# Keys and queries moved to whole heads for the attention scores of six local-attention layers, values kept as copied

## The chip, the cores and the metric

The kernel runs on one core of a Trainium2 chip. The metric is the device time of one execution in microseconds (us), the lower the better. Everything is float32 unless marked otherwise.

## The reference, cut to what matters

The program has two blocks. The first one is a test-time-training layer followed by a stack of six transformer layers; the second is an attention with relative positions and a mixture of experts. The change touches only the six transformer layers, for 4 sequences of 512 tokens of width 128, 16 heads of width 64 and windows of 32 tokens:

```python
for i in range(DEPTH):                       # 6
    x = attn_layer(shift_tokens(x), Wqkv[i], q_scale[i], k_scale[i], Wo[i]) + x
    x = ffn_layer(shift_tokens(x), ln_g[i], ln_b[i], W1[i], b1[i], W2[i], b2[i]) + x
...
q = l2norm(q) * qs;  k = l2norm(k) * ksc
q = q * cos * scale + rotate_half(q) * sin * scale
k = k * cos * inv + rotate_half(k) * sin * inv
# local_attention: a window of 32 queries against its own and the previous 32 keys
sim = jnp.einsum('bhwie,bhwje->bhwij', bq, bk2) * QK_SCALE
sim = jnp.where(mask, -jnp.finfo(sim.dtype).max, sim)
out = jnp.einsum('bhwij,bhwje->bhwie', jax.nn.softmax(sim, -1), bv2)
```

## The kernel before

**Units, rounds, parts.** One pair of layer and sequence is a *unit* (24 of them, `u`), 32 rounds apart; `rounds` (L719) is an order written out by hand, and each engine walks it in order: in round `r` it does step `s = r - 32u` of every unit that is alive, and of every *part* (a tile of 128 tokens and half of the heads, 8 parts a unit, 192 in all, 4 rounds apart from step 39 on). So at any time the projections of unit `u` stand beside the attention of unit `u-1` and the feed-forward of `u-1` or `u-2`. Steps below are counted from a unit's start. A part's step 0 falls on 39, 43, ... 67; seen from the next unit these are 7, 11, ... 35, and the last part's and the one before it on 35 and 31.

**Projections and rotation, steps 0 to 35.** For each of the 8 groups `p` of 4 heads (keys 0 to 3, queries 4 to 7) TensorE makes two halves of 128 columns (L1111 to L1113): rows 32j to 32j+31 hold the lower (or the upper) half of head j. ScalarE squares them (L1293), VectorE multiplies by the rotary tables (L1421, four operations), GpSimd sums the squares (L1556) and joins the rotated parts (L1562, L1563, signal `made`) right in `kT` or `qT`. The norms of the keys are inverted by VectorE at step 17 and those of the queries at step 33 (`inverse_root`, L217 to L226), the keys' ones go out to DRAM and come back spread over 32 rows a head (`norms_wide`, L957), and VectorE scales the keys in place (L1444, steps 24, 28, 29, 32, signal `k_scaled`).

**Scores.** A head's two halves of 32 rows lie in one place, `[32j, g, half]`, so `part_tensor` takes two matmuls of 32 rows for each window and head, the second added in PSUM (L1211): 64 matmuls a part. In the trace each float32 matmul shows as two instructions, so 128.

**Softmax and values.** VectorE multiplies the scores by the queries' norms (L1486) and takes the largest (L1491); ScalarE takes the exponentials (L1357, 8 operations), VectorE inverts the sums (L1494, part step 3), GpSimd scales (L1577), TensorE turns (L1219, part step 5) and weighs the values (L1229, part step 6, 32 matmuls of tiles 64x64), then mixes the heads (L1237). The values come out of the projection by token (steps 29 to 55), ScalarE copies them to `v_tok` (L1306), and SyncE lays the windows out with 8 or 10 DMAs a tile (`value_windows`, L972 to L977).

**Queues.** All DMAs of the layers are issued by SyncE, in the order of `transformer_sync`, waits included: what stands behind a waiting entry waits too. The feed-forward of a unit follows its last part (steps 80 to 109), and the next layer's shift of the same sequence stands at step 124.

## Time and profile before

| | us |
|---|---|
| median of 3 runs (lowest, highest) | 2512.24 (2499.67, 2514.59) |
| the profiled execution's own time | 2506.73 |
| its span, first to last instruction | 2504.8 |

The profiled execution is 5.5 us below the median and within the spread of the three. Spans, idle times and chains in the rows below are all of that one execution. The engines are PE (TensorE), PEld (its weight loads), DVE (VectorE), ACT (ScalarE), POOL (GpSimd) and SP (SyncE); SPq is SyncE issuing DMAs. "Idle before" is the time in which an engine stood still right before a group of instructions, with what released it.

### The profile page before, as it was taken

The numbers are of one execution on the slowest core, as the hardware profiler recorded it, in microseconds if no ns is written. First come the engines' busy times: TensorE is split into PE (matmuls) and PEld (weight loads), VectorE is DVE, ScalarE is ACT, GpSimd is POOL, SyncE is SP. The second block draws the span as 40 slices with busy tenths as digits, with TensorE's granted clock in tenths as the row PEclk, the third lists the DMA queues.
The fourth block names the chain that finished last, engine by engine and source line by source line (L and its number), as shares of the span: only waits on it lengthen the run. The fifth ranks groups of instructions, "written<-read, shape, count | busy, mean of one in ns | idle before, by whom it ended". The sixth has DMA issues, their size and how long they took to land.

```text
span 2504.8 us, 121652 instructions
## 1 busy us (share of the span) xinstructions
PE 2354.9 (94%) x53677; PEld 1748.5 (70%) x53677; DVE 1717.0 (69%) x3393; ACT 1597.2 (64%) x5036; POOL 1451.3 (58%) x1408
## 2 busy tenths in 40 slices
PE   9958999999999999999999999999888999999967
PEld 8836777777777777677777777777645666666657
DVE  4477788777888888787788788887335555555534
ACT  3226777777777787777777778777625454545422
POOL 1166667656676676566666677665117656656307
PEclk9969999999999999999999999999979999999978
DMA  4013333433333334333343333333216222222136
GB/s 91 15 33 86 79 83 94 97 80 83 91 93 95 82 83 103 83 92 87 80 96 90 80 92 87 87 87 87 54 30 177 49 48 48 48 48 48 31 97 249
DMA packets 230208, 204.60 MB, mean 82 GB/s; under 512 B 133687, under 2 KB 155464, under 8 KB 229552
## 3 DMA queue, kind: packets, MB, share of 16 engines
q1 hardware_dynamic: 225296, 190.91, 30.5%
q8 instruction: 422, 6.91, 1.2%
q0 software_dynamic: 2208, 5.58, 0.7%
q14 instruction: 106, 0.87, 0.1%
q10 hardware_dynamic: 2176, 0.33, 0.1%
HBM read 86.05 MB, written 15.70 MB: 41 GB/s over the span
## 4 chain that ended last, share of the span: by engine, by line
PE 66%; DVE 12%; SPq 6%; ACT 5%; issue 5%; POOL 4%; DMA 3%; POOLq 0%; ACTq 0%; DVEq 0%
PE psum L1211 7%; PE psum L1959 5%; PE psum L1237 5%; PE psum L1229 5%; PE psum L1938 4%; PE psum L1111 4%; PE psum L1944 3%; PE psum L1113 3%; PE psum L1112 3%; PE psum L1993 3%; PE psum L1983 3%; ACT p L1357 3%; SPq L972 3%; PE psum L1188 2%; PE psum L1219 2%
## 5 line engine op out<-in xcount | busy, mean ns | idle before, releaser
L1357 ACT ACTIVATE p<-p,stat 128x64 f32<-128x64 f32 x1536 | 512.4, 336 | 47.2 <-DVE stat L1491 44.9
L1577 POOL TENSOR_TENSOR p<-p,inverse 128x512 f32<-128x512 f32 x192 | 200.2, 1043 | 456.5 <-DVE inverse L1494 452.2
L1211 PE MATMUL psum<-kT,qT 32*32 32x64 f32 x24576 | 305.5, 224 | 25.8 <-issue 24.2
L2092 DVE TENSOR_REDUCE largest<-psum 128x1 f32<-128x512 f32 x256 | 165.0, 687 | 228.0 <-PE psum L1944 228.0
L1211 PEld LDWEIGHTS psum<-kT,qT 32*32 32x32 f32 x24576 | 264.1, 103 | 75.3 <-issue 74.3
L1357 ACT ACTIVATION_READ_ACCUMULATOR p<-p,stat 128x1 f32 x1536 | 288.6, 188 | 0.0
L1421 DVE SCALAR_TENSOR_TENSOR rotated<-psum,scales,rotary 128x512 f32<-128x512 f32 x384 | 270.8, 742 | 25.8 <-ACT sq L1293 25.8
L1556 POOL TENSOR_TENSOR squares<-sq 128x512 f32<-128x512 f32 x192 | 245.3, 1278 | 44.3 <-ACT sq L1293 43.8
L1293 ACT ACTIVATE sq<-psum 128x512 f32<-128x512 f32 x384 | 213.7, 582 | 57.3 <-PE psum L1113 54.6
L1229 PEld LDWEIGHTS psum<-pT,v_win 64*64 64x64 f32 x12288 | 198.6, 136 | 64.7 <-issue 45.9
L1111 PE MATMUL psum<-xs,wqkv_high 128*128 128x512 f32 x384 | 205.7, 536 | 23.2 <-DVE rotated L1421 22.9
L2014 ACT ACTIVATE w_by_key<-psum 128x512 f32<-128x512 f32 x128 | 76.4, 597 | 230.1 <-PE psum L1959 230.1
L1229 PE MATMUL psum<-pT,v_win 64*64 64x32 f32 x12288 | 220.1, 221 | 2.8 <-ACT pT L1363 1.8
L1237 PEld LDWEIGHTS psum<-oT,wo 128*128 128x128 f32 x1536 | 187.9, 196 | 38.5 <-issue 26.3
L1237 PE MATMUL psum<-oT,wo 128*128 128x128 f32 x1536 | 198.2, 283 | 9.0 <-ACT oT L1368 5.6
L1363 ACT ACTIVATE pT<-psum 128x512 f32<-128x512 f32 x192 | 114.2, 595 | 130.4 <-PE psum L1219 130.3
L1306 ACT ACTIVATE v_tok<-psum 128x512 f32<-128x512 f32 x192 | 113.8, 593 | 101.8 <-PE psum L1113 73.9
L1444 DVE TENSOR_TENSOR kT<-kT,rnorm_wide 128x1024 f32<-128x1024 f32 x96 | 164.0, 1728 | 13.4 <-DMA rnorm_wide<-rnorms 13.3
L2104 POOL TENSOR_TENSOR q_by_head<-q_heads,mask_head 64x256 fp32r<-64x256 f32 x252 | 157.5, 625 | 15.4
L2060 ACT ACTIVATE weights<-psum,largest 128x512 f32<-128x512 f32 x256 | 161.5, 687 | 3.7 <-DVE largest L2092 3.7
L1421 DVE SCALAR_TENSOR_TENSOR kT<-psum,scales,rotary 128x512 f32<-128x512 f32 x192 | 142.3, 741 | 28.2 <-ACT sq L1293 14.4
L1563 POOL TENSOR_TENSOR qT<-qT,rotated 128x512 f32<-128x512 f32 x96 | 157.9, 1645 | 0.0
(351 smaller groups left out, 5402.3 us busy)
## 6 DMA issues: line engine op xcount, KB each, us to landing
v_win<-v_tok SPq DMA_DIRECT2D x576, 128.0 KB
rnorm_wide<-rnorms SPq DMA_DIRECT2D x384, 64.0 KB
v_win<-v_tok SPq DMA_DIRECT2D x336, 64.0 KB
q_rows<-q_rows_all SPq DMA_DIRECT2D x32, 512.0 KB, 4.6
tile_weights<-expert_table SPq DMA_DIRECT2D x23, 512.0 KB, 5.8
wqkv<-L_ffn_Wqkv SPq DMA_DIRECT2D x96, 64.0 KB, 2.2
rel_values<-sq SPq DMA_DIRECT2D x60, 64.0 KB, 2.2
wo<-L_ffn_Wo SPq DMA_DIRECT2D x48, 64.0 KB
```

What stands on the lines that cost most here:

```text
L1111: PE.e.matmul(out, w[0], x[1], start=True, stop=False)
L1211: last = PE.e.matmul(psum[WIN * blk:WIN * (blk + 1), f, out], q[rows, g, half, tok:tok + WIN], k[rows, g, half, tok:tok + 2 * WIN], start= ...
L1229: last = PE.e.matmul(psum[to:to + DH, 2 + o, at:at + WIN], v[rows, blk, 2 * (2 * a + o) + h, :], t.pt[h][rows, 2 * a + o, blk * WIN:(blk + ...
L1237: last = PE.e.matmul(ps[:, 0:P], t.wo[:, e, :], t.ot[e % 2][:, e // 2, :], start=(e == 0), stop=(e == PAIRS - 1))
L1293: A.e.activation(t.sq[half][:, :], c.psum[:, 4 + half, :], ACT.Square).then_inc(*t.squared.by((u, (p, half))))
L1357: last = A.e.activation(p, p, ACT.Exp, bias=t.stat[:, h, 2 * g + f:2 * g + f + 1], accum_out=t.sum[:, h, g, f:f + 1])
L1421: last = V.e.scalar_tensor_tensor(out=rot[x], in0=psum[:, 4 + half, :], scalar=scale, in1=table, op0=ALU.mult, op1=ALU.mult)
L1444: V.e.tensor_tensor(k, k, t.wide[g % 2][:, :].unsqueeze(1).to_broadcast([P, 2, S]), ALU.mult).then_inc(*t.k_scaled.by((u, g)))
L1556: G.e.tensor_tensor(t.sq_both[p % 2][:, :], t.sq[0][:, :], t.sq[1][:, :], ALU.add).then_inc(*t.squares.by((u, p)))
L1577: G.e.tensor_tensor(p, p, t.inv[:, h, :, :].unsqueeze(3).to_broadcast([P, GROUPS_TF, 2, 2 * WIN]), ALU.mult).then_inc(*t.p_scaled.by(m))
L2060: A.e.activation(t.e[n % 4][:, :], c.psum[:, n % 5, :], ACT.Exp, bias=t.mx[n % 4][:, 0:1]).then_inc(*t.exped.by(n))
L2092: V.e.tensor_reduce(t.mx[n % 4][:, :], psum[:, n % 5, :], AX, ALU.max, negate=True).then_inc(*t.largest.by(n))
```

## The change

- **Scores over 64 rows.** `q` and `k` now hold whole heads: rows 64f to 64f+63 are one head, both halves. A window and head takes one matmul of 64 rows and 32 columns of weights: 32 a part. Which of two banks a head's scores go to depends on the window too (`swapped`).
- **Staging and relay.** Rotated queries are made in six staging buffers, and the keys' scaling writes its product there, one operation for each half. `relay` moves each group's two halves from staging to the whole heads with 4 DMAs (64 rows of 2 KB each) on SyncE: 8 relays a unit. The first score of a unit waits for the last of them; VectorE waits for a relay six buffers back before it writes a staging buffer.
- **Norms.** One DMA instead of four spreads the norms of a group. The steps of spreading and scaling move (the third scaling from 29 to 32, the last from 32 to 33, behind the queries' `inverse_root` of step 33).
- **Values.** ScalarE copies the values straight into `v_win`; odd windows use that copy as it is, the others a second copy made by 4 or 6 DMAs a tile. For that, half of the heads' values come from tokens whose 64-halves are exchanged (`swap_halves`: four copies on GpSimd at step 28). The order of the weighing matmuls follows `swapped`. Values move from steps 29 to 33, their DMAs from 31 to 37.
- **The rest.** The feed-forward starts 4 steps later; the copy of the queries' norms takes 3 operations; squares use three buffers; `pT` has one.

```diff
--- before.py
+++ after.py
@@ -712,20 +712,21 @@
-VALUE_FIRST, WINDOWS_AT = 29, 31
+VALUE_FIRST, WINDOWS_AT, SWAP_AT = 33, 37, 28
 SHIFT_AT = -4
-SQUARES_LAG, SUM_LAG, MADE_LAG = 2, 4, 3
-NORM_AT = {"root0": 17, "out": 15, "root1": 33, "turn": 39, "copy": 39}
-SPREAD_AT = (16, 18, 19, 24)
-SCALE_AT = (24, 28, 29, 32)
+SQUARES_LAG, SUM_LAG, MADE_LAG, RELAY_LAG = 2, 4, 3, 4
+NORM_AT = {"root0": 17, "out": 19, "root1": 33, "turn": 39, "copy": 39}
+SPREAD_AT = (20, 20, 26, 29)
+SCALE_AT = (24, 28, 32, 33)
+STAGES, WIDES = 6, 2
...
-FFN_AT = {"shift": 80, "center": 83, "square": 84, "sum": 84, "root": 84, "spread": 88, "scale": 89, "gate0": 91, "gate1": 95, "gate2": 96, "gelu": 99,
-          "up0": 100, "up1": 101, "up2": 104, "down": 108, "add": 109}
+FFN_AT = {"shift": 84, "center": 87, "square": 88, "sum": 88, "root": 88, "spread": 92, "scale": 93, "gate0": 95, "gate1": 99, "gate2": 100, "gelu": 103,
+          "up0": 104, "up1": 105, "up2": 108, "down": 112, "add": 113}
 NORM_SPREAD, NORM_SCALE = 2, {1: 9, 2: 17, 3: 25}
 NORM_ENDS = (0, B - 1)
 TABLES = (2, 3, 0, 1)
-UNIT_STEPS = 110
-SPLIT_AT = {2: 13, 3: 31, 0: 39, 1: 40, 4: 56, 5: 59}
+UNIT_STEPS = 118
+SPLIT_AT = {2: 13, 3: 31, 0: 39, 1: 40, 4: 60, 5: 62}
...
+def swapped(f, blk):
+
+    return f if blk < TPB // 2 else 1 - f
+
+
+def squares_at(u, p, half=0):
+
+    return (2 * GROUPS_TF * u + p + half) % 3
+
+
+def stage_of(u, kind, g, half):
+
+    turn = [(1, 0), (1, 1), (0, 0), (1, 2), (0, 1), (1, 3), (0, 2), (0, 3)].index((kind, g))
+    return (2 * GROUPS_TF * u + turn) * 2 + half
+
+
+def relayed_on(t, k):
+
+    return t.relayed[k % STAGES].on((k, 1))
+
+
 def made_of(t, u, kind, g):

-    return [t.q[u % 2][:, g, half, :] if kind else t.k[u % 2][:, g, half, WIN:WIN + S] for half in range(2)]
+    if kind:
+        return [t.stage[stage_of(u, 1, g, half) % STAGES][:, :] for half in range(2)]
+    return [t.k[u % 2][:, g, half, WIN:WIN + S] for half in range(2)]
...
+            for g in range(GROUPS_TF):
+                if s == 4 * (GROUPS_TF + g) + RELAY_LAG:
+                    SP.wait_ge(*t.made.on((u, GROUPS_TF + g)))
+                    relay(c, t, u, 1, g)
+                if s == SCALE_AT[g] + 1:
+                    SP.wait_ge(*t.k_scaled.on((u, g)))
+                    relay(c, t, u, 0, g)
...
 def norms_wide(c, t, u, g):

+    SP, x = c.SP, GROUPS_TF * u + g
+    SP.wait_ge(*t.rn_out.on(u))
+    if x >= WIDES:
+        SP.wait_ge(*t.k_scaled.on(divmod(x - WIDES, GROUPS_TF)))
+    src = bass.AP(t.rn_dram[u % 2].tensor, g * S, [[GROUPS_TF * S, 4], [0, HALF_D], [1, S]])
+    SP.e.dma_start(t.wide[x % WIDES][:, :], src).then_inc(*t.wide_in[x % WIDES].by(x))
+
+
+def relay(c, t, u, kind, g):
-    SP.wait_ge(*t.rn_out.on(u))
-    if u or g >= 2:
-        SP.wait_ge(*t.k_scaled.on((u, g - 2) if g >= 2 else (u - 1, GROUPS_TF + g - 2)))
-    for j in range(4):
-        src = bass.AP(t.rn_dram[u % 2].tensor, (j * GROUPS_TF + g) * S, [[0, HALF_D], [1, S]])
-        SP.e.dma_start(t.wide[g % 2][HALF_D * j:HALF_D * (j + 1), :], src).then_inc(*t.wide_in[g % 2].by((u, g, j)))
+    if u >= 2:
+        SP.wait_ge(*t.scored.on((u - 1) * PARTS - 1))
+    for half in range(2):
+        k = stage_of(u, kind, g, half)
+        for e in range(2):
+            to = t.q[u % 2][half::2, g, e, :] if kind else t.k[u % 2][half::2, g, e, WIN:WIN + S]
+            SP.e.dma_start(to, t.stage[k % STAGES][e * H64:(e + 1) * H64, :]).then_inc(*t.relayed[k % STAGES].by((k, e)))


...
-    SP, v, vt, v_in = c.SP, t.v[n % 2], t.vt[n % 2], t.v_in[n % 2]
+    SP, v, before, v_in = c.SP, t.v[n % 2], t.v[(n - 1) % 2], t.v_in[n % 2]
     SP.wait_ge(*t.v_kept.on((n, 1)))
     if n >= 2:
         SP.wait_ge(*t.weighted.on(2 * (n - 2) + 1))
-    k = 0
-    for f in range(2):
-        at = f * 2 * WIN
-        for blk in range(1, TPB):
-            SP.e.dma_start(v[at:at + 2 * WIN, blk, :, :], vt[(blk - 1) * WIN:(blk + 1) * WIN, f, :, :]).then_inc(*v_in.by((n, k)))
-            k += 1
-        SP.e.dma_start(v[at + WIN:at + 2 * WIN, 0, :, :], vt[0:WIN, f, :, :]).then_inc(*v_in.by((n, k)))
-        k += 1
-        if n % TPB:
-            SP.e.dma_start(v[at:at + WIN, 0, :, :], t.vt[(n - 1) % 2][P - WIN:P, f, :, :]).then_inc(*v_in.by((n, k)))
-            k += 1
+    w0, w1, w2, w3 = (slice(WIN * w, WIN * (w + 1)) for w in range(TPB))
+    SP.e.dma_start(v[WIN:P, 1, 0, :, :], v[0:P - WIN, 0, 0, :, :]).then_inc(*v_in.by((n, 0)))
+    SP.e.dma_start(v[w1, 1, 1, :, :], v[w0, 0, 1, :, :]).then_inc(*v_in.by((n, 1)))
+    SP.e.dma_start(v[w0, 1, 1, :, :], v[w3, 0, 1, :, :]).then_inc(*v_in.by((n, 2)))
+    SP.e.dma_start(v[w3, 1, 1, :, :], v[w2, 0, 1, :, :]).then_inc(*v_in.by((n, 3)))
+    if n % TPB:
+        SP.e.dma_start(v[w0, 1, 0, :, :], before[w3, 0, 0, :, :]).then_inc(*v_in.by((n, 4)))
+        SP.e.dma_start(v[w2, 1, 1, :, :], before[w1, 0, 1, :, :]).then_inc(*v_in.by((n, 5)))
...
+        if f:
+            PE.wait_ge(*t.swapped.on(u))
+        tokens = [x[:, i * P:(i + 1) * P] for x in (t.xp if f else xs)]
+        three_products(PE, ps, tokens, w).then_inc(*t.valued.by((u * TPB + i, f)))
...
-        PE.wait_ge(*t.k_scaled.on((u, GROUPS_TF - 1)))
-        PE.wait_ge(*t.made.on((u, 2 * GROUPS_TF - 1)))
+        for back in range(STAGES):
+            PE.wait_ge(*relayed_on(t, 4 * GROUPS_TF * (u + 1) - 1 - back))
...
-            for half in range(2):
-                for blk in range(TPB):
-                    tok, out = i * P + blk * WIN, slice(g * 2 * WIN, (g + 1) * 2 * WIN)
-                    for f in range(2):
-                        j = 2 * h + f
-                        rows = slice(HALF_D * j, HALF_D * (j + 1))
-                        last = PE.e.matmul(psum[WIN * blk:WIN * (blk + 1), f, out], q[rows, g, half, tok:tok + WIN], k[rows, g, half, tok:tok + 2 * WIN],
-                                           start=False, stop=(half == 1 and g == GROUPS_TF - 1))
+            for blk in range(TPB):
+                tok, out = i * P + blk * WIN, slice(g * 2 * WIN, (g + 1) * 2 * WIN)
+                for f in range(2):
+                    rows = slice(DH * f, DH * (f + 1))
+                    last = PE.e.matmul(psum[WIN * blk:WIN * (blk + 1), swapped(f, blk), out], q[rows, g, h, tok:tok + WIN], k[rows, g, h, tok:tok + 2 * WIN],
+                                       start=False, stop=(g == GROUPS_TF - 1))
...
-                        rows, to, at = slice(DH * f, DH * f + DH), (f + o) % 2 * DH, a * P + blk * WIN
-                        last = PE.e.matmul(psum[to:to + DH, 2 + o, at:at + WIN], v[rows, blk, 2 * (2 * a + o) + h, :],
-                                           t.pt[h][rows, 2 * a + o, blk * WIN:(blk + 1) * WIN], start=True, stop=True)
+                        slot, to, at = swapped(f, blk), (f + o) % 2 * DH, a * P + blk * WIN
+                        rows = slice(DH * slot, DH * slot + DH)
+                        last = PE.e.matmul(psum[to:to + DH, 2 + swapped(o, blk), at:at + WIN], v[rows, 1 - blk % 2, f, 2 * (2 * a + o) + h, :],
+                                           t.pt[rows, 2 * a + o, blk * WIN:(blk + 1) * WIN], start=True, stop=True)
...
-        A.e.activation(t.rq[u % 2][:, :, :].rearrange("p b r -> p (b r)"), ring_bank(c, t, "unit", u, "rn")[:, 0:P], ACT.Copy).then_inc(*t.rn_kept.by(u))
+        norms = ring_bank(c, t, "unit", u, "rn")[:, 0:P]
+        A.e.activation(t.rq[u % 2][0:H64, :, :].rearrange("p b r -> p (b r)"), norms[0:H64, :], ACT.Copy)
+        pairs = lambda x: x.rearrange("p (b a h f g) -> p b a h f g", b=TPB, a=2, h=2, f=2)
+        for f in range(2):
+            last = A.e.activation(pairs(t.rq[u % 2][H64:P, :, :].rearrange("p b r -> p (b r)"))[:, :, 1, :, 1 - f, :], pairs(norms[H64:P, :])[:, :, 1, :, f, :], ACT.Copy)
+        last.then_inc(*t.rn_kept.by(u))
...
+        if kind:
+            for half in range(2):
+                if stage_of(u, kind, g, half) >= STAGES:
+                    V.wait_ge(*relayed_on(t, stage_of(u, kind, g, half) - STAGES))
...
-    if s in SCALE_AT:
-        g = SCALE_AT.index(s)
-        k = t.k[u % 2][:, g, :, WIN:WIN + S]
-        V.wait_ge(*t.wide_in[g % 2].on((u, g, 3)))
-        V.wait_ge(*t.made.on((u, g)))
-        V.e.tensor_tensor(k, k, t.wide[g % 2][:, :].unsqueeze(1).to_broadcast([P, 2, S]), ALU.mult).then_inc(*t.k_scaled.by((u, g)))
+    for g in range(GROUPS_TF):
+        if s == SCALE_AT[g]:
+            x = GROUPS_TF * u + g
+            V.wait_ge(*t.wide_in[x % WIDES].on(x))
+            V.wait_ge(*t.made.on((u, g)))
+            for half in range(2):
+                k = stage_of(u, 0, g, half)
+                if k >= STAGES:
+                    V.wait_ge(*relayed_on(t, k - STAGES))
+                last = V.e.tensor_tensor(t.stage[k % STAGES][:, :], t.k[u % 2][:, g, half, WIN:WIN + S], t.wide[x % WIDES][:, :], ALU.mult)
+            last.then_inc(*t.k_scaled.by((u, g)))
...
+    if s == SWAP_AT:
+        if u:
+            G.wait_ge(*t.valued.on((u * TPB - 1, 1)))
+        for k in range(2):
+            for to, x in swap_halves(t, u, k):
+                last = G.e.tensor_copy(to, x)
+        last.then_inc(*t.swapped.by(u))
```

## Rows read from the trace of the kernel before

**Rows 1.** The page: busy time by engine, and the chain that ended last

```profile
PE 2354.9 (94%) x53677; PEld 1748.5 (70%) x53677; DVE 1717.0 (69%) x3393; ACT 1597.2 (64%) x5036; POOL 1451.3 (58%) x1408
...
PE 66%; DVE 12%; SPq 6%; ACT 5%; issue 5%; POOL 4%; DMA 3%; POOLq 0%; ACTq 0%; DVEq 0%
```

**Rows 2.** Busy time by stretch, 600 to 1400 us (inside the layers)

```profile
core 0: us, PE busy (x) PEld busy (x) DVE busy (x) ACT busy (x) POOL busy (x), PEclk, DMA share, GB/s
600.00:1400.00 800.00, 777.63 (x21274) 582.74 (x21257) 645.90 (x1263) 619.02 (x2149) 531.39 (x417) 1.00 0.36 90
```

**Rows 3.** One line's instructions: the copy of norms, one a unit

```profile
L1298 ACT ACTIVATE rnorm_tok<-psum x24: 268/278/280, 188.3 to 1753.1; 128x128 f32<-128x128 f32 x24
```

**Rows 4.** Groups by line, 600 to 1400 us: count | busy us, mean ns | idle before

```profile
L1211 PE MATMUL psum<-kT,qT 32*32 32x64 f32 x11995 | 148.5, 223 | 10.9 <-issue 10.0
...
L1229 PE MATMUL psum<-pT,v_win 64*64 64x32 f32 x5952 | 105.7, 220 | 0.9 <-issue 0.9
```

**Rows 5.** Instructions of L1211 within 904.6 to 905.2 us

```profile
L1211 PE MATMUL psum<-kT,qT x58: 212/214/238, 904.6 to 905.2; 32*32 32x64 f32 x58
```

**Rows 6.** PE in order of time: start us, length us, what

```profile
913.04 1.48 PE L1211 MATMUL psum<-kT,qT 32*32 32x64 f32 x128
914.45 1.12 PE L1180 MATMUL psum<-sq,w 128*128 128x512 f32 x2
...
918.97 1.14 PE L1229 MATMUL psum<-pT,v_win 64*64 64x32 f32 x64
920.04 0.50 PE L1111 MATMUL psum<-xs,wqkv_high 128*128 128x512 f32 x1
...
926.02 0.66 PE L1219 MATMUL psum<-ident,p 128*128 128x128 f32 x4 [1.01 <-POOL p L1577]
...
931.57 0.39 PE L1203 MATMUL psum<-maskb,identb 128*128 128x256 bf16 x2
```

**Rows 7.** DVE in order of time, steps 27 to 34 of one unit

```profile
907.04 0.68 DVE L1486 TENSOR_TENSOR p<-psum,rnorm_tok 128x512 f32<-128x512 f32 x1
909.07 0.29 DVE L1498 TENSOR_TENSOR z<-z,psum 128x128 f32<-128x128 f32 x1 [1.34 <-PE psum L1237]
...
909.87 4.20 DVE L1444 TENSOR_TENSOR kT<-kT,rnorm_wide 128x1024 f32<-128x1024 f32 x2
913.99 0.19 DVE L1494 RECIPROCAL inverse<-sum 128x8 f32<-128x8 f32 x1
...
918.01 1.22 DVE L1444 TENSOR_TENSOR kT<-kT,rnorm_wide 128x1024 f32<-128x1024 f32 x1
919.14 0.28 DVE L1431 TENSOR_TENSOR norms<-psum,norms 128x128 f32<-128x128 f32 x1
...
924.64 0.20 DVE L1494 RECIPROCAL inverse<-sum 128x8 f32<-128x8 f32 x1
```

**Rows 8.** ACT: the last of eight exponentials between those two inverses

```profile
912.47 0.34 ACT L1357 ACTIVATE p<-p,stat 128x64 f32<-128x64 f32 x1
```

**Rows 9.** POOL: joining group 6 (step 27), scaling; then all casts of L2161

```profile
908.44 1.28 POOL L1563 TENSOR_TENSOR qT<-qT,rotated 128x512 f32<-128x512 f32 x1
...
924.92 1.04 POOL L1577 TENSOR_TENSOR p<-p,inverse 128x512 f32<-128x512 f32 x1 [3.28 <-DVE inverse L1494]
...
L2161 POOL CAST keys<-k x16: 396/448/507, 1870.9 to 2322.5; 128x256 fp32r<-128x256 f32 x8, 128x384 fp32r<-128x384 f32 x8
```

**Rows 10.** SyncE issuing DMAs, in order of time

```profile
904.05 2.19 SPq L972 DMA_DIRECT2D v_win<-v_tok  x3
...
907.56 2.69 SPq L972 DMA_DIRECT2D v_win<-v_tok  x3
...
910.93 0.59 SPq L977 DMA_DIRECT2D v_win<-v_tok  x1
...
922.69 2.78 SPq L972 DMA_DIRECT2D v_win<-v_tok  x3
```

**Rows 11.** DMAs issued, 600 to 1400 us: count, KB each, us to landing

```profile
v_win<-v_tok SPq DMA_DIRECT2D x280, 128.0 KB
...
wqkv<-L_ffn_Wqkv SPq DMA_DIRECT2D x48, 64.0 KB, 2.2
```

**Rows 12.** PE near the end of the layers, in order of time

```profile
1828.95 2.07 PE L1173 MATMUL psum<-ident,rstd 128*128 128x128 f32 x8 [2.42 <-DVE rstd L226]
1832.38 5.49 PE L1180 MATMUL psum<-sq,w 128*128 128x512 f32 x6 [1.36 <-DVE sq L1459]
```

79 lines of the change are left out of this document (44 added, 35 removed).

## The prediction

> **What bounds the kernel now.** First the page: TensorE is busy for 94% of the span and carries 66% of the chain that ended last; the reader is to see that no other engine carries more than 12% of it [rows 1]. Then the layers alone, from 600 to 1400 us: of 800 us TensorE is busy 777.6 (97%), VectorE 645.9 (81%), ScalarE 619.0 (77%), GpSimd 531.4 (66%), the DMA engines 36%, at a granted clock of 1.00, which is the 2.4 GHz level [rows 2]. So the layers are bound by TensorE on average, but VectorE has only a fifth of its time left. The period of a unit is (1753.1 - 188.3) / 23 = 68.0 us [rows 3], and 24 units make nearly 1640 us: 1 us a unit is 24 us, almost 1% of the whole.
>
> Then one unit in order of time, because the shares hide where the slack lies. In steps 27 to 34 VectorE lags: the third and second scaling take 4.20 us together beside GpSimd's work, against 1.22 us for one that runs alone, and the queries' inverse root runs from about 919.4 to 924.6 [rows 7]. Only then comes the inverse of a part's sums at 924.64, GpSimd's scaling at 924.92 [rows 9], and TensorE's turn at 926.02, for which it stood still for 1.01 us [rows 6]. From that turn to the next unit's first score, at 931.57, TensorE needs 5.55 us [rows 6]. I call steps 27 to 39 the heavy half (score 27 to score 39); the rest of the unit has room beside TensorE.
>
> **The change, part by part.** *Scores.* 11995 instructions are 93.7 parts; their 148.5 us busy and 10.9 us of waits for instructions make 1.70 us a part [rows 4], 1.41 at least (913.04 to 914.45) [rows 6]. The new part has 64 instructions. Bounds: 64 instructions at the rate of the first 58 of an old part, 0.6 us [rows 5], or half of 1.41, 0.70; above, what the 64 instructions of the weighing take, 1.07 (918.97 to 920.04) [rows 6], with weights of 64 columns, where the new scores keep 32. Moving columns (64) and tiles in use at once (8) stay as they are, so I take 0.85, nearer the lower end, and leave half of the 0.29 us of excess, 0.15: 1.00. Saved: 0.70 us a part.
>
> *Weighing.* Same 32 matmuls, but `swapped` turns their order round after the second window: the tile used last is wanted again at once, three times a part. The rows show no such case. Below it costs nothing (the same tiles and columns); above, each waits for one whole round of four tiles, 1.07 / 8 = 0.13, so 0.4. It could gain nothing, since no operand shrinks. I take 0.10, nearer nothing, for two instructions of a tile already follow each other. Net on TensorE: 0.60 us a part, 4.8 a unit, 115 in all, if all of it reached the end.
>
> Here the trace leaves something open: the weighing lets two row tiles write to one bank, in different rows, and its 64 instructions still take 17 ns each [rows 6], but this may be its weights' loading or that sharing. The Trainium skill, TensorEngine Tiling (Array Packing), Restrictions and Gotchas, says that different row tiles can't access one PSUM bank at the same time. The old scores kept each row tile to its own bank; the new ones let both into each. By that rule the new part would not reach 0.85; it is the third rival below.
>
> *VectorE.* Two scalings of 512 columns for one of 1024: at least 1.22 us, at most half of 4.20 = 2.10 [rows 7]; I take 1.7 for a pair. In the unit shown: the mix ends 0.75 earlier (one shorter score ahead of it), so the sum z starts at 908.3 and the maximum ends at 909.2; one scaling instead of two ends at 910.9; the exponentials, which ended at 912.8 [rows 8], end 0.7 sooner, so the inverse stands at 912.3 instead of 913.99 [rows 7]. From there the old order runs 4.0 us to the scaling at 918.01: 916.3. The third scaling (now step 32) ends at 918.0, the norms and the inverse root last 5.5 (919.14 to 924.64): 923.5. The last scaling, now behind the root, ends at 925.2, and the part's inverse comes at 925.3, 0.7 later than before. GpSimd and the turn follow: 926.7, plus 5.55 = 932.3 for the first score, against 931.57 [rows 6]. So the heavy half gains nothing and loses about 0.7 us, although TensorE has three shorter scores in it. What hid VectorE there was TensorE's own work; the cover is gone. Between 930.5 (every scaling at 1.22) and 933.2 (at 2.1) lies -1.1 to +1.6.
>
> *GpSimd.* The exchange at step 28 is four copies of 128x256, 0.45 us each by the casts of such tiles [rows 9], 1.6 to 2.1 us. It stands behind group 6's joining, which ends at 909.7, and ahead of the next unit's shift; a part's scaling would run from about 915 instead of 914.3. Behind it wait the joining of group 7 and its relay, and the turn of step 32: 1 us late for TensorE, which catches up before the turn of step 36 that waits anyway. It costs nothing extra.
>
> *SyncE and DMA.* A unit issues 32 relay DMAs, 4 for norms, 22 for values and 1: 59, before 16 + 38 + 1 = 55. From step 28 to the first score, 27 come in one row: relays of queries 2 (4), values (6), keys 1 (4), norms (1), queries 3, keys 2, keys 3 (12). Ten such issues took 904.05 to 911.52, 0.75 us each [rows 10]; 27 take 20.2 from 909.7 (joining of group 6 done) [rows 9]: 929.9. A DMA lands 2.2 us after its issue starts [rows 11], so 1.6 after the issue ends: 931.5, just ahead of the 932.3 of VectorE's path. It is hidden by 0.8 us. Bytes: values from 992 KB a tile to about 480, relays add 4.2 MB a unit; net +2 MB on 6.1, with the engines 36% busy [rows 2], so some 48% after: no bound. Value DMAs at step 37 instead of 31 still stand 8 steps ahead of their use.
>
> *Light half.* Five scores of the eight lie in it (39 to 55). 5 x 0.60 = 3.0 us saved, at TensorE's pace, since VectorE, ScalarE and GpSimd have room there. The copies on ScalarE for the norms (two more, at most 0.28 each [rows 3]) hide.
>
> *Ends.* Four more steps leave part of one feed-forward uncovered at the end (stalls of 2.42 and 1.36 us show how thin work is there [rows 12]); the first unit waits for its relays. 3 us in all, 0 to 8.
>
> **Sum.** Unit: -3.0 + 0.7 = -2.3; 24 units: -55; ends +3: -52. From the profiled execution's own 2506.7 that is 2455; the median of the runs is 5.5 above that execution, so 2460 for the median.
>
> **The rivals.**
> 1. *All of TensorE's saving arrives*: VectorE's path in the heavy half is not the tight one, because its waits shrink too. For it: 97% busy TensorE, a stall of only 1.01 us at the turn. Against it: the sum above. 24 x 4.8 = 115, +3: 2395 + 5.5 = 2400.
> 2. *The relays come late*, and the kernel gets slower. Place: SyncE's 27 issues ahead of step 39. Three issues of 64 rows have taken 2.78 us, 0.93 each [rows 10]; if all were like these, 909.7 + 25.0 + 1.6 = 936.3, 4.7 later than 931.57. The unit changes by 4.7 - 3.0 = +1.7: +41, +3: 2551, with the 5.5, 2556. It decides from where the last relay lands 3 us after 931.57, at 0.87 us an issue. Against it: ten issues in a row averaged 0.75.
> 3. *Row tiles in one bank exclude each other.* Every second pair of windows would wait for the pair ahead: 0.35 us more a part in the scores and weighing. Light half 5 x 0.25 = 1.25, less 0.7: -0.55 a unit, -13, +3: 2497, with the 5.5, 2502. This is the rule of the Trainium skill named above (TensorEngine Tiling, Gotcha 1). For it: 17 ns an instruction in the weighing. Against it: weights of 64 columns explain these as well.
> 4. *The change doesn't do what it says*, for the halves are twice handled: excluded as a whole by the instruction counts, which the diff fixes; that its cover fails in small places (exchange, ring of squares, one `pT`) gives about 2500.
>
> **How the numbers follow.** Chances: the forecast 0.45, rival 1 0.20, rival 2 0.14, rival 3 0.13, rival 4 0.08. About 1% (25 us) is what a measurement of this kernel can tell from no change, so faster means below 2487 and slower above 2537. Faster: forecast 0.43, rival 1 0.20, rival 3 0.03: 0.66. Slower: rival 2 beyond 2537, 0.13. Same: the rest, 0.21. The range reaches from rival 1 (2400, less 5 for its own spread) to 2515, past rivals 3 and 4; outside are rival 2 and the lucky end of rival 1. The forecast's own range, from the heavy half's -1.1 to +1.6 us and a part's saving of 0.45 to 0.75, is 2420 to 2500.
>
> **What would show it.** Right: 64 instructions a part at about 0.85 us; a unit of 65.7 us; TensorE busy some 93% in the layers instead of 97%, standing still for 2 to 3 us before the turn of step 36 (released by GpSimd's scaling behind VectorE's inverse); VectorE near 84%; the last relay landing shortly before the first score. Wrong: the first score released by a DMA (rival 2), scores of over 1.1 us a part (rival 3), a TensorE still 97% busy with a unit near 63 us (rival 1). The sum would fail most easily at the light half, if there, too, the chain score, maximum, exponentials, inverse, scaling, turn left no room once TensorE is quicker.

## The result, and the profile after

| | before | after |
|---|---|---|
| median of 4 runs each (lowest, highest), us | 2510.60 (2499.67, 2514.59) | 2760.84 (2759.70, 2768.23) |
| span of the profiled execution, us | 2504.8 | 2759.1 |
| granted clock of TensorE, mean | 0.966 | 0.917 |

The ratio is 1.101, 95% interval 1.097 to 1.105: the changed kernel is 10% slower, +250 us, or 10.4 us for each of the 24 units. The prediction had 2460 us. Below, one point is 1% of the time before, 25 us; gains and losses are given in points of the ratio to the kernel before on the same chip, because its median moved by 0.6% between the groups of runs (2495.2 to 2511.0). One execution of e12 and one of e16 were in a slower state and are left out of medians and ratios.

The page of the kernel after: busy time by engine, then the chain that ended last. It answers [rows 1].

```profile
PE 2360.0 (86%) x41389; PEld 1701.2 (62%) x41389; DVE 1720.7 (62%) x3489; ACT 1607.0 (58%) x5106; POOL 1457.0 (53%) x1503
...
PE 37%; ACT 15%; DVE 13%; SPq 12%; DMA 10%; POOL 7%; issue 5%; another core or an unknown queue 0%; ACTq 0%; DVEq 0%; POOLq 0%
```

Every engine is busy for almost the same time as before, in a span 254 us longer. TensorE had 66% of the chain and has 37%; what it lost went to ScalarE, to SyncE's issues and to DMAs in flight. So no engine became the bound: the engines wait for each other.

The same in the layers (busy time by stretch, columns as in [rows 2]), and one stretch of 5 us inside them:

```profile
600.00:1400.00 800.00, 685.61 (x13183) 490.72 (x13182) 556.40 (x1131) 540.62 (x1894) 459.61 (x398) 0.91 0.42 102
940.00:945.00 5.00, 0.84 (x4) 0.84 (x5) 1.35 (x3) 2.47 (x5) 1.28 (x1) 0.56 0.72 195
```

TensorE is busy for 686 us of 800 instead of 778, the granted clock is 0.91 instead of 1.00. It fell where TensorE stood: from 940 to 945 us it worked for 0.84 of 5 us, and the mean grant was 0.56. TensorE stood from 939.6 to 944.2; the grant was 0.80 from 940 to 941, 0.50 (the level of 1.2 GHz) from 941 to 947, and 1.00 again from 948.

TensorE's work is thus stretched too. Its busy time of 2360.0 us looks like that of before, but it now has 41389 matmul instructions instead of 53677. The kernel of e4 below has the same 41389 and is busy for 2233.0 us, at a mean grant of 0.971 instead of 0.917. So up to 127 us of TensorE's busy time in after are work at the lower clock. How much of that reaches the end was not measured, and each price below contains its share of it.

TensorE in order of time around the scores of one part (`L1262`) and a weighing (`L1281`), which answer [rows 6]:

```profile
890.51 1.14 PE L1281 MATMUL psum<-pT,v_win 64*64 64x32 f32 x64
891.58 0.50 PE L1155 MATMUL psum<-xs,wqkv_high 128*128 128x512 f32 x1
...
892.70 0.86 PE L1262 MATMUL psum<-kT,qT 64*32 64x64 f32 x64
893.49 0.33 PE L1190 MATMUL psum<-ident,rnorm 128*128 128x128 f32 x1
```

And the new copies of norms, two a unit, from which the period of a unit follows as in [rows 3]:

```profile
L1362 ACT ACTIVATE rnorm_tok<-psum x48: 179/187/194, 194.4 to 2004.1; 64x32 f32<-64x32 f32 x48
```

(2004.1 - 194.4) / 23 = 78.7 us a unit, before 68.0. The 10.7 us are the result: (78.7 - 68.0) x 24 = 257 us, about the whole of the 254 us that the span grew. The loss lies in every unit, not at the ends.

What the engines wait for, 600 to 1400 us (engine, line, what it waited for: us in all, times, the longest):

```profile
ACT v_win L1372 <- DMA v_win<-v_win: 51.0, 10, 6.5
...
PE psum L1289 <- ACT oT L1435: 35.0, 10, 5.1
...
DVE stage L1519 <- DMA rnorm_wide<-rnorms: 9.7, 10, 2.7
...
PE psum L1256 <- DMA kT<-stage: 6.8, 3, 3.3
```

Some ten units lie in that stretch. Once a unit ScalarE waits 5 us for the DMAs that lay out the tile of values before, and TensorE 3.5 us at the mix for ScalarE's copy (`oT`) that stands behind. Before, the same wait was

```profile
ACT v_tok L1306 <- DMA v_win<-v_tok: 11.7, 6, 4.1
```

The first score of a unit, `L1256`, is held by a relay only three times (6.8 us). The chain of the work that ended last, in one of those places (start us, us, what):

```profile
925.96 1.24 POOL stage L1643
927.22 0.53 SPq L1004
...
930.90 0.58 SPq L990
...
932.19 0.59 SPq L1016
...
934.81 0.59 SPq L1021
935.44 6.99 DMA v_win<-v_win
...
959.32 5.34 DMA rnorm_wide<-rnorms
```

GpSimd joins a group of queries, SyncE issues its relay (`L1004`), the spreading of norms (`L990`) and the windows of a tile of values (`L1016` to `L1021`), which then take 7.0 us to land. The stretch in which the clock fell, 940 to 945 us, is the one in which ScalarE waits for them and TensorE for ScalarE (in order of time; the bracket is idle time before, with what ended it):

```profile
939.18 0.39 PE L1157 MATMUL psum<-wqkv_high,x_swapped 128*128 128x512 f32 x1
944.16 3.59 PE L1289 MATMUL psum<-oT,wo 128*128 128x128 f32 x16 [4.59 <-ACT oT L1435]
```

A DMA of norms takes 5.3 us. The prediction had given a landing 2.2 us [rows 11].

### The profile page after: what moved, and what is told of

Its sections match the earlier page's. It is cut to its first block, busy times and chain, and to the rows that moved or that the text cites. A ratio compares the mean times of both kernels' runs of the same rounds, so it can differ in the third digit from the quotient of the medians.

```text
span 2759.1 us, 97721 instructions
## 1 busy us (share of the span) xinstructions
PE 2360.0 (86%) x41389; PEld 1701.2 (62%) x41389; DVE 1720.7 (62%) x3489; ACT 1607.0 (58%) x5106; POOL 1457.0 (53%) x1503
## 4 chain that ended last, share of the span: by engine, by line
PE 37%; ACT 15%; DVE 13%; SPq 12%; DMA 10%; POOL 7%; issue 5%; another core or an unknown queue 0%; ACTq 0%; DVEq 0%; POOLq 0%
ACT p L1424 6%; SPq L1004 6%; DMA v_win<-v_win 5%; PE psum L2039 5%; PE psum L2018 4%; DMA rnorm_wide<-rnorms 3%; PE psum L2024 3%; DVE rotated L1492 3%; PE psum L1289 3%; PE psum L2073 3%; PE psum L2063 3%; PE psum L1235 2%; POOL stage L1642 2%; POOL stage L1643 2%; ACT sq L1353 1%
## 5 line engine op out<-in xcount | busy, mean ns | idle before, releaser
L1289 PE MATMUL psum<-oT,wo 128*128 128x128 f32 x1536 | 231.4, 313 | 97.6 <-ACT oT L1435 92.6
L1289 PEld LDWEIGHTS psum<-oT,wo 128*128 128x128 f32 x1536 | 217.7, 224 | 128.9 <-ACT oT L1435 112.8
L1281 PEld LDWEIGHTS psum<-pT,v_win 64*64 64x64 f32 x12288 | 210.8, 143 | 78.1 <-issue 46.0
L1155 PE MATMUL psum<-xs,wqkv_high 128*128 128x512 f32 x384 | 221.4, 576 | 28.9 <-DVE rotated L1492 28.5
L1281 PE MATMUL psum<-pT,v_win 64*64 64x32 f32 x12288 | 232.5, 227 | 9.4 <-ACT pT L1430 9.4
L1270 PE MATMUL psum<-ident,p 128*128 128x128 f32 x768 | 130.3, 296 | 116.9 <-POOL p L1657 61.6
L1372 ACT ACTIVATE v_win<-psum 128x512 f32<-128x512 f32 x192 | 114.6, 597 | 158.9 <-DMA v_win<-v_win 118.8
L1570 DVE RECIPROCAL inverse<-sum 128x8 f32<-128x8 f32 x192 | 38.3, 199 | 252.8 <-ACT p L1424 252.8
L1270 PEld LDWEIGHTS psum<-ident,p 128*128 128x128 f32 x768 | 95.9, 153 | 160.2 <-POOL p L1657 154.6
L1519 DVE TENSOR_TENSOR stage<-kT,rnorm_wide 128x512 f32<-128x512 f32 x192 | 170.7, 930 | 29.2 <-DMA rnorm_wide<-rnorms 29.0
L1353 ACT ACTIVATE sq<-psum 128x512 f32<-128x512 f32 x256 | 147.1, 584 | 45.7 <-PE psum L1157 43.7
L1262 PE MATMUL psum<-kT,qT 64*32 64x64 f32 x12288 | 168.1, 227 | 0.0
```

The costliest lines, as they stand in the source:

```text
L1155: PE.e.matmul(out, w[0], x[1], start=True, stop=False)
L1262: last = PE.e.matmul(psum[WIN * blk:WIN * (blk + 1), swapped(f, blk), out], q[rows, g, h, tok:tok + WIN], k[rows, g, h, tok:tok + 2 * WIN] ...
L1270: last = PE.e.transpose(psum[:, 2, g * P:(g + 1) * P], t.p[h][:, g, :, :].rearrange("p f k -> p (f k)"), c.ident[:, :])
L1281: last = PE.e.matmul(psum[to:to + DH, 2 + swapped(o, blk), at:at + WIN], v[rows, 1 - blk % 2, f, 2 * (2 * a + o) + h, :], t.pt[rows, 2 * a ...
L1289: last = PE.e.matmul(ps[:, 0:P].rearrange("p (x q) -> p x q", x=2), t.wo[:, e, :], mixed_rows(t, e % 2, e // 2), start=(e == 0), stop=(e = ...
L1353: A.e.activation(t.sq[squares_at(u, p, half)][:, :], c.psum[:, 4 + half, :], ACT.Square).then_inc(*t.squared.by((u, (p, half))))
```

## The experiments

Eighteen kernels with edits, all on one core. One unit's 8 parts start at steps 7, 11, ... 35 of the next unit. Behind the experiments stands a table of the mean time from each part's first mask matmul (`L1203`) to the next one's. It is worked out from the starts of those instructions over 20 units.

### The norms in one DMA

The kernel after, with the norms of a group spread by four DMAs as before:

```diff
-    src = bass.AP(t.rn_dram[u % 2].tensor, g * S, [[GROUPS_TF * S, 4], [0, HALF_D], [1, S]])
-    SP.e.dma_start(t.wide[x % WIDES][:, :], src)...
+    for j in range(4):
+        src = bass.AP(t.rn_dram[u % 2].tensor, (j * GROUPS_TF + g) * S, [[0, HALF_D], [1, S]])
+        SP.e.dma_start(t.wide[x % WIDES][HALF_D * j:HALF_D * (j + 1), :], src)...
```

> The kernel after with one edit: the norms of a group are spread by four DMAs of 32 rows each, as in the kernel before, instead of by one whose source has the dimensions 4, 32, 512. Same bytes, three more issues of about 0.45 us for each group on SyncE. Theory A (the one norms DMA is served by few DMA engines, so it lands after 5 us, and whatever stands behind it in their rings lands late too: the 7.0 us landing of the value windows and the 5.3 us landing of the norms in the chain of the kernel after): the 10 us a unit that were lost come back, about 2480 us (2440 to 2530). Theory B (the 32 relay DMAs a unit and their 4.2 MB fill the rings, whatever form the norms take): no gain, 2740 to 2800 us, for SyncE issues 12 DMAs a unit more.

The opposite, the kernel before with one DMA for a group:

> The kernel before with one edit: the norms of a group are spread by one DMA with the dimensions 4, 32, 512, as in the kernel after; steps, scores and values stay. Theory A: slower than before though SyncE has 12 issues a unit less, by the share of the loss that doesn't need relays behind it: 2550 to 2700 us. Theory B: 2500 to 2515 us, no change or slightly faster.

Measured: after with four, 2706.0 us, ratio 1.085 (1.082 to 1.087), where after has 1.101: 1.6 points, 41 us, come from this one DMA. That is a sixth of the loss, where theory A expected all of it and theory B none. Before with one: 2515.7 us, 1.009 (1.006 to 1.013), 23 us slower although it issues 12 DMAs less a unit, so B is out and A's 2550 to 2700 us is missed too. A stretch of that kernel in which a DMA of norms was all that was in flight (columns as in [rows 2]):

```profile
975.00:976.00 1.00, 0.63 (x24) 0.59 (x25) 1.00 (x2) 0.86 (x4) 0.00 (x0) 1.00 0.26 102
```

The DMA engines' share is 0.26, about 4 of 16. The source pattern is [4, 32, 512]: the Trainium skill, DMA: Bandwidth & Descriptors, How many engines (k), says that a DMA is laid on the largest number of engines, up to 16, that divides the slowest dimension of its source and of its target, and this row agrees for 4. No run here has the same bytes with the dimensions in another order. VectorE pays, in that kernel and in the one before (waits, 600 to 1400 us):

```profile
DVE kT L1443 <- DMA rnorm_wide<-rnorms: 27.8, 19, 2.7
```

```profile
DVE kT L1444 <- DMA rnorm_wide<-rnorms: 6.6, 6, 1.6
```

Why it costs 41 us in after and 23 in before was not measured. In after the relays and the DMAs of values stand behind it in a longer row; whether they queue on the same four engines is open.

### The scores alone

The kernel before with only its loop of scores changed (heads come out mixed: the data stays where it was, the shapes are those of after):

```diff
-            for half in range(2):
-                ... rows = slice(HALF_D * j, HALF_D * (j + 1)); matmul(..., q[rows, g, half, ...], k[rows, g, half, ...])
+                    rows = slice(DH * f, DH * (f + 1))
+                    last = PE.e.matmul(psum[WIN * blk:WIN * (blk + 1), f, out], q[rows, g, h, tok:tok + WIN], k[rows, g, h, tok:tok + 2 * WIN], ...)
```

> The kernel before with only the scores changed: 32 matmuls of 64 rows a part instead of 64 of 32 rows, each row tile in its own bank as before. It leaves out the move to whole heads, so it multiplies rows of different heads and its result is another one; the work of every other engine and all waits stay. It measures what TensorE's saving is worth with nothing added. If all of it arrives (0.62 us a part by the trace of the kernel after, where 64 instructions and the way to the next take 0.79 us against 1.41): 192 x 0.65 = 125 us less, 2385 us. If VectorE's path through steps 27 to 39 sets that half, as predicted: five of eight parts, 75 us less, 2435 us.

Measured: 2456.3 us, 0.984 (0.982 to 0.986): 1.6 points, 40 us. The group of scores and the waits, 600 to 1400 us:

```profile
L1209 PE MATMUL psum<-kT,qT 64*32 64x64 f32 x6208 | 83.5, 224 | 0.0
```

```profile
PEld psum L1217 <- POOL p L1575: 42.3, 36, 2.3
PEld psum L1235 <- ACT oT L1366: 40.1, 48, 1.4
```

97 parts at 0.86 us, against 148.5 / 93.7 = 1.58 [rows 4], and 10.9 / 93.7 = 0.12 us of waits for instructions are gone too. Neighbouring groups overlap, so TensorE's busy time falls by less, by 122 us in the whole kernel (2354.9 to 2233.0) or 0.64 a part. With the waits that is about 0.75 a part, near the 0.70 predicted, and 145 us over 192 parts; a good quarter of it arrives. Both expectations, all of it (2385 us) and five eighths (2435 us), are missed.

TensorE now stands at the turn (`L1217`) for GpSimd's scaling and at the mix (`L1235`) for ScalarE's copy, and not only in the heavy half: by the starts in the trace, over 20 units, 3.8 of these 7.1 us a unit lie before step 27. So the chain scores, maximum, exponentials, inverse, scaling, turn, with the mix behind it, limits TensorE in the light half too. That it does so in every part isn't shown: the turn waits 36 times in 97 parts.

### The relays

The kernel with four DMAs of norms (e1), without relays from the third unit on; with relays of 64 columns instead of 512; with half of each relay's DMAs:

```diff
+                if u >= 2:
+                    continue            # e5
...
+            n = S if u < 2 else 64      # e6
...
-        for e in range(2):
+        for e in range(2 if u < 2 else 1):   # e7
```

> The kernel of e1 (norms in four DMAs) without relays and without waits for them from the third unit on; it leaves out the move of keys and queries to whole heads there, so its scores are those of stale rows. Everything else of the change stays: 64-row scores, exchange on GpSimd, values straight into their windows, queries' norms ahead of the last scaling. Theory C (SyncE's one queue: 32 relay issues a unit stand ahead of norms and value windows, and those come late): nearly all of e1's loss goes, 2450 to 2490 us. Theory E (the direct copy of values, which now waits for the previous tile's windows five steps after their issue, or the exchange on GpSimd, or the scaling behind the root, is itself the loss): 2550 to 2700 us.

> The kernel of e1 with all its relays issued and waited for, but from the third unit on with 64 instead of 512 columns a row: the same number of issues and packets, an eighth of the bytes; most of each row isn't moved, so the scores are wrong. Theory C (issue time on SyncE): as e1, 2690 to 2715 us. Theory D (the bytes in the DMA rings, landing late): as e5.

> The kernel of e1 with two of the four DMAs of each relay from the third unit on: half of the issues and half of the bytes, one half of the heads isn't moved. Theory C: 16 issues of 0.65 us less in a unit whose queue is the chain; half of the loss against e5 or more goes, 2540 to 2620 us, and clearly below e6. Theory D: between e6 and e1, no lower than e6.

With all relays of queries issued by GpSimd, right behind its joining:

> The kernel of e1 with the queries' relays (16 DMAs a unit) issued by GpSimd right behind the operation that makes them, the keys' still by SyncE; all of the result is computed. Theory C: SyncE's queue is relieved of half of the relays, 2550 to 2650 us, unless GpSimd's own issue (about 1 us each for the indirect DMAs it issues in the last stage) delays its scalings; then 2650 to 2800 us. Theory D: as e1, 2690 to 2715 us.

Measured: without relays 2654.8 us, 1.064 (1.062 to 1.065), 2.1 points or 53 us less than e1's 1.085. Short relays 2689.7, 1.078 (1.076 to 1.080): the bytes are 0.7 points, the issues and their places the rest. Half the DMAs 2657.8, 1.065 (1.062 to 1.068): the second half, issues and bytes, costs 49 us, the first 4. So it isn't a fixed price per DMA. That everything behind the row is late from some length on fits this, and no run varied the length further. Moving the queries' issues to GpSimd, 2697.9, 1.081 (1.079 to 1.083), takes back 0.4 points.

Theory C (SyncE's row) has the direction in e5 to e7 and too much of the size: of the 216 to 256 us it expected in e5, 53 came, and e7 and e8 miss its ranges as well. Theory E (another part of the change is the loss; 2550 to 2700 us in e5) fits e5, and the next two groups of runs follow it. Theory D (the bytes alone) is out by e6. In e1, where the norms' DMA is no longer in the way, the relays do hold the first score of nearly every unit; in e8 no engine waits for a relay or a window any more, and TensorE waits for GpSimd's scaling instead, for GpSimd is busy for 563 us of 800 there and 479 in e1 (waits, 600 to 1400 us: e1, e1, e8):

```profile
PE psum L1257 <- DMA kT<-stage: 20.2, 9, 4.4
PE psum L1271 <- POOL p L1658: 23.6, 15, 2.6
```

```profile
PE psum L1274 <- POOL p L1664: 60.5, 25, 5.6
```

### The exchange of the values' halves

e5 with `swap_halves` for the first unit only:

```diff
-    if s == SWAP_AT:
+    if s == SWAP_AT and u == 0:
```

> The kernel of e5 (no relays from the third unit on, norms in four DMAs) that also exchanges the halves of the tokens only for the first unit, so half of the values of later units come from stale tokens. Theory G (GpSimd's four copies at step 28, 1.6 us in e5's trace, stand with the shift of 2.3 us ahead of a part's scaling and make TensorE wait): 2590 to 2620 us against e5's 2655. Theory F (the later feed-forward and values set the loss): no more than 10 us less, 2645 to 2655 us.

Measured: 2617.3 us, 1.049 (1.048 to 1.051): 1.4 points, 36 us, or 1.5 us a unit. The four copies in e5 (lines, 600 to 1400 us: count | busy, mean ns):

```profile
L1635 POOL CAST x_swapped<-xs 128x256 fp32r<-128x256 f32 x44 | 20.4, 503 | 0.0
```

They take 0.50 us each, 2.0 a unit, and 1.5 us a unit reach the end, as theory G expected (2590 to 2620 us).

### What is left: later steps alone, in the kernel before

e9 is still 4.9 points, 123 us, slower than before, with shorter scores, without relays and exchange. What remains of the change are steps in other places. Each was made alone in the kernel before:

```diff
-FFN_AT = {"shift": 80, "center": 83, ...}; SPLIT_AT = {..., 4: 56, 5: 59}
+FFN_AT = {"shift": 84, "center": 87, ...}; SPLIT_AT = {..., 4: 60, 5: 62}     # e10
-VALUE_FIRST, WINDOWS_AT = 29, 31
+VALUE_FIRST, WINDOWS_AT = 33, 37                                             # e11: e10 and this
-SPREAD_AT = (16, 18, 19, 24); SCALE_AT = (24, 28, 29, 32); "out": 15
+SPREAD_AT = (20, 21, 26, 29); SCALE_AT = (24, 28, 32, 33); "out": 19          # e12 (the second spreading at 21; after has 20)
```

> The kernel before with only the feed-forward's steps 4 later and the last two weight splits at 60 and 62, as in the kernel after. Theory F1 (the gelu, with its two table loads 4.2 us on ScalarE, now falls on step 103, a round that is also a unit's first score with the copy of its norms, and the exponentials behind it come late): slower than before, 2560 to 2620 us. Otherwise within 10 us of 2497 us.

> The kernel before with the steps of the change for values (33, their DMAs 37) and for the feed-forward, nothing else: same operations, same DMAs. Theory F2 (the schedule itself, values and feed-forward together, is the loss, because their copies now meet the exponentials): 2600 to 2660 us, most of what e5 has over before. If the direct copy of values and the exchange are the loss: below 2540 us.

> The kernel before with only the steps of the norms moved as in the change: the DMA out at 19, their spreading at 20, 21, 26, 29, the scalings at 24, 28, 32, 33, the last behind the queries' inverse root. The prediction's own term: the part's inverse 0.7 us later in the heavy half, TensorE not faster here: 0.5 to 1.5 us a unit, 2510 to 2535 us. If VectorE's order doesn't matter: 2490 to 2505 us.

| kernel before with | us | ratio (95%) |
|---|---|---|
| feed-forward 4 later, splits moved (e10) | 2690.0 | 1.079 (1.077 to 1.081) |
| that, and values at 33, their DMAs at 37 (e11) | 2868.9 | 1.150 (1.148 to 1.153) |
| scalings late, nearly as in after (e12) | 2504.8 | 1.004 (1.003 to 1.005) |

The edit that the prediction put at nothing but "ends" is the largest of those made alone, and larger than expected (2560 to 2620 us). Values late cost 7 points more in the old arrangement, with its 38 window DMAs a unit, again beyond what was expected (2600 to 2660 us); ScalarE's copy of values waits 131 us of 800 for these DMAs there. In after there are 22, and what moving the values costs there was not measured alone. The scalings cost 10 us, 0.4 a unit, below the 0.5 to 1.5 expected.

### Which part of the feed-forward's move

The steps of the feed-forward 4 later, the splits where they were; 8 later; 4 later with the queries' norms turned and copied at step 37 instead of 39, and that same step in e1:

```diff
-FFN_AT = {"shift": 80, ... "gelu": 99, ...}
+FFN_AT = {"shift": 84, ... "gelu": 103, ...}     # e13
+FFN_AT = {"shift": 88, ... "gelu": 107, ...}     # e15
-"turn": 39, "copy": 39
+"turn": 37, "copy": 37                           # e14: e13 and this; e16: e1 and this
```

> The kernel before with the feed-forward 4 steps later and nothing else (weight splits stay at their steps; in e10 they moved too, to 60 and 62, behind the point at which values at step 29 need them). Theory H (the gelu's 4.2 us on ScalarE meets the queries' norms and a unit's first score on step 39): most of e10's loss stays, 2590 to 2650 us. Theory I (in e10 the splits that came late were the loss, about 8 us at each of five layer borders and more behind them): below 2530 us.

> The kernel of e13 with the turn and the copy of the queries' norms at step 37 instead of 39, so ahead of the gelu on ScalarE. Theory H in its narrow form (VectorE's first scores and TensorE's ring wait for that copy behind the gelu, 1.9 and 2.4 us in the trace of e10): 50 to 90 us less than e13. If the exponentials behind the second table load are what is late: no more than 20 us less.

> The kernel before with the feed-forward 8 steps later instead of 4, nothing else. The mixes and the sums of squares come every 8 steps, so against them it stands as before, and its gelu falls on step 107, so 43, away from the copy of the norms. Theory H: within 30 us of the kernel before, 2490 to 2525 us. If any later feed-forward costs because its work meets other parts: 2600 us or more.

> The kernel of e1 (the change with the norms in four DMAs) with the turn and the copy of the queries' norms at step 37, all of the result computed. Theory H, narrow: 30 to 90 us less than e1's 2706, 2620 to 2675 us. If exponentials or SyncE's queue set the end there anyway: 2690 us or more.

| kernel | us | ratio (95%) |
|---|---|---|
| before, feed-forward 4 later (e13) | 2675.8 | 1.066 (1.064 to 1.068) |
| e13 and norms copied at 37 (e14) | 2677.6 | 1.065 (1.063 to 1.067) |
| before, feed-forward 8 later (e15) | 2600.7 | 1.035 (1.034 to 1.037) |
| e1 and norms copied at 37 (e16) | 2722.0 | 1.084 (1.082 to 1.086) |

Four steps later costs 6.6 points, 165 us, eight steps only 3.5: the tail isn't it, for it would grow. It is the neighbourhood. The other 1.3 points of e10 are the splits of the weights, which come too late there for values at step 29 at each of the five layer borders (e10, 600 to 1400 us, three borders):

```profile
PE psum L1111 <- POOL wqkv_low L1569: 21.0, 3, 7.3
```

ScalarE in e13, in order of time (start us, us, what), with the gelu at its new step 103, which is step 39 of the unit after the next:

```profile
1006.84 1.28 ACT L1345 ACT_TABLE_LOAD   x1
1008.14 1.67 ACT L1345 ACTIVATE act<-act 128x512 f32<-128x512 f32 x3
1009.71 0.25 ACT L1298 ACTIVATE rnorm_tok<-psum 128x128 f32<-128x128 f32 x1
...
1011.38 0.58 ACT L1363 ACTIVATE pT<-psum 128x512 f32<-128x512 f32 x1
1011.98 1.28 ACT L1357 ACT_TABLE_LOAD   x1
```

TensorE and VectorE in the same stretch; the bracket is idle time before, with what ended it:

```profile
1010.02 1.12 PE L1183 MATMUL psum<-sq,w 128*128 128x512 f32 x2 [2.38 <-ACT rnorm_tok L1298]
```

```profile
1010.00 0.69 DVE L1486 TENSOR_TENSOR p<-psum,rnorm_tok 128x512 f32<-128x512 f32 x1 [1.85 <-ACT rnorm_tok L1298]
```

The copy of the norms stands behind a gelu that holds ScalarE for 4.2 us (a table load, three operations, and the load back, 1.28 + 1.67 + 1.28), and both others wait for that copy. It looks like the cause, and the copy's place isn't: with the copy 2 steps earlier (e14, e16) nothing is gained (the intervals overlap, at most 0.4 points). The wait goes, and another takes its place. Theory H is thus out, also by e15, which it put within 30 us of before. After has the same place, and the same two engines stand (ScalarE, then VectorE):

```profile
896.01 1.28 ACT L1412 ACT_TABLE_LOAD   x1
897.30 1.67 ACT L1412 ACTIVATE act<-act 128x512 f32<-128x512 f32 x3
```

```profile
899.46 0.69 DVE L1562 TENSOR_TENSOR p<-psum,rnorm_tok 128x512 f32<-128x512 f32 x1 [1.67 <-ACT rnorm_tok L1362]
```

In the kernel before the gelu stood 4 steps earlier, at step 99, 35 of the unit after the next:

```profile
922.92 1.28 ACT L1345 ACT_TABLE_LOAD   x1
924.22 1.67 ACT L1345 ACTIVATE act<-act 128x512 f32<-128x512 f32 x3
...
927.33 1.28 ACT L1357 ACT_TABLE_LOAD   x1
```

from 922.9 to 928.6 us, beside the inverse root of VectorE (919.5 to 924.6, [rows 7]) and the turn that waits for it [rows 6]. That stretch is long anyway. The theory then (J in the expectations): two long pieces of work, of ScalarE and of VectorE, shared one part's interval, and now each has one of its own.

### The gelu without its table loads

If that is so, the loads must be nearly free at the old step and dear at the new one. The same kernels with a plain copy in the gelu's place, which needs no load and leaves out only the gelu's function:

```diff
-            ... t.act[0:n, j, :], t.act[0:n, j, :], ACT.Gelu)
+            ... t.act[0:n, j, :], t.act[0:n, j, :], ACT.Copy)
```

> The kernel before with a plain copy in place of the gelu (three operations of the same size; the result leaves the gelu out), so that ScalarE loads no table, 2 x 1.28 us less a unit, 61 us in all. Theory J (in the kernel before the gelu on step 99, so 35, shares one part's interval with VectorE's inverse root of step 33, and the two long stretches hide each other): little of it arrives, 0 to 30 us less, 2475 to 2505 us. Theory K (the loads always stand on the path): 55 to 65 us less.

> The kernel of e13 (feed-forward 4 steps later) with the same copy in place of the gelu. Theory J: the stretch of 4.2 us on ScalarE stands alone here, ahead of a unit's first exponentials, so the whole of the two loads and more (waits of TensorE on the ring behind it) comes back: 60 to 120 us less than e13's 2676. Theory L (what costs is only who follows whom in the ring of two PSUM banks): no more than in e17.

> The kernel of e9 (the change without relays, without exchange, norms in four DMAs; stale rows as there) with the same copy in place of the gelu. Theory J: its 120 us over the kernel before are the feed-forward's place, so 55 to 100 us less than e9's 2617. Theory L: no more than in e17.

| kernel | with gelu | with copy | the loads' price, points |
|---|---|---|---|
| before | 1.000 | 0.998 (0.997 to 0.999) | 0.2 |
| feed-forward 4 later (e13, e18) | 1.066 | 1.044 (1.041 to 1.046) | 2.2 |
| e9 (e19) | 1.049 | 1.030 (1.028 to 1.032) | 1.9 |

The same 24 pairs of loads, 61 us of ScalarE's time, cost 5 us at one step and 56 us four steps later; in the kernel after without relays and exchange 48 us. That part is shown, and theory L is out; both later prices lie just under theory J's ranges (60 to 120 and 55 to 100 us). That it is VectorE's inverse root which hides the loads at the old step was not tested: no run moved it.

The other 4.4 points of e13 are not separated by runs, but the trace of e13 names a second wait of the same size. TensorE's waits, 600 to 1400 us:

```profile
PE psum L1111 <- ACT v_tok L1306: 27.6, 11, 3.8
PE psum L1183 <- ACT rnorm_tok L1298: 24.9, 11, 2.4
```

of which the kernel before has 4.3 and nothing. The second stands behind the gelu, and in e18 it shrinks. The first is still there in e18:

```profile
PE psum L1111 <- ACT v_tok L1306: 28.3, 14, 4.0
PE psum L1183 <- ACT rnorm_tok L1298: 8.9, 11, 1.0
```

TensorE waits in `L1111` for a bank that ScalarE's copy of values has to empty, and that copy waits for the DMAs of windows (41.2 us of 800 in e13, 11.7 in before). The chain behind one such place in e13, in order of time:

```profile
1046.54 1.20 DVE root_t L217
...
1050.65 1.23 DVE kT L1444
1051.89 0.30 SPq L957
...
1061.18 2.04 DMA v_win<-v_tok
1063.31 0.61 ACT v_tok L1306
1063.95 0.80 PE psum L1111
```

The feed-forward's own inverse root (4.2 us of VectorE) has moved from step 84 to 88, which is 24 of the unit after the next, and now stands right ahead of the first scaling of keys. SyncE waits for that scaling in the middle of its row of 12 norm DMAs, and the windows stand behind it. The row in e13 and in before:

```profile
1041.96 11.63 SPq L957 DMA_DIRECT2D rnorm_wide<-rnorms  x12
```

```profile
896.20 7.75 SPq L957 DMA_DIRECT2D rnorm_wide<-rnorms  x12
```

By the starts in the trace this wait costs TensorE 2.2 us a unit, in 19 of 20 units between the scores of steps 31 and 35, and the one behind the gelu 2.2 us between 7 and 11; e13 is 6.9 us a unit slower. So the move met two neighbours, not one. No run took the second one away alone.

### One part to the next

Mean us from a part's first mask matmul to the next part's, named by the step numbers of the next unit. The last column is their sum, a unit:

```
step         7-11 11-15 15-19 19-23 23-27 27-31 31-35  35-7   sum
before        7.1  10.4   6.4   9.6   7.1   8.9   8.8  10.0  68.2
e4            6.7  10.7   5.6   8.8   7.4   7.9   9.3  10.1  66.4
e13          11.7   8.4   9.1   7.8   8.6   8.8  11.4   9.5  75.4
e15          10.0   9.5   7.3  10.3   6.3   9.7  10.4   9.1  72.5
e18           9.6   8.4   9.0   7.8   8.6   9.0  10.7   9.6  72.7
e9           12.0   7.9   9.1   6.9   9.5   8.3  10.2   9.8  73.7
e19          10.0   7.7   9.0   6.9   9.8   8.2  10.1   9.7  71.3
e5           11.3   7.9   9.0   6.9   9.6   8.3  12.8   9.4  75.3
e1            9.6   7.9   9.0   6.9   9.8  12.3   9.0  12.5  77.1
after        11.0   7.9   9.2   6.9   9.5  14.6   8.3  11.9  79.4
```

In e13 and e9 the interval 7-11, where the gelu now stands (39 is 7 of the next unit; in before it is 35-7), goes from 7.1 to about 12 us, and 35-7 gains next to nothing (10.0 to 9.5 and 9.8). Without the loads (e18, e19) 7-11 falls by 2.1 and 2.0 us. The 2.6 us more of e13 in 31-35 are the wait for the windows. The exchange is the interval 31-35 (e5 against e9, +2.6), the relays 27-31 and 35-7 (e1 against e5, +4.0 and +3.1, given back partly in 7-11 and 31-35), the norms' DMA 27-31 (+2.3).

From before to after: feed-forward later and shorter scores, with all other moves, +4.9 points (e9); exchange +1.4; relays +2.1; norms' DMA +1.6; 10.1 in all, in that order of putting them in. Inside the 4.9, e13 times e4 gives 1.066 x 0.984 = 1.049, just e9, but that is no proof that the feed-forward's move is all of it. In e9 no engine waits for a DMA between 600 and 1400 us, so e13's wait for the windows isn't in it, and other parts of the change must make up for that. Shown in the changed kernel itself are the exchange, the relays, the norms' DMA and the loads' 1.9 points, 7.0 of 10.1 in all; that the rest is the feed-forward's place too is argued from the kernel before.

## Why the prediction was wrong

**Right.** The new score part: from 892.70 to 893.49 us, 0.79, against 0.85 predicted, and 0.62 less than the shortest old one, 1.41. The weighing needs 890.51 to 891.58, 1.07, as before: the turned order doesn't cost the 0.10 taken for it. Scores that put both row tiles into each bank (after) and scores that keep a bank for each (e4) both take 0.86 us, so rival 3 is out. TensorE does stand before the turn, and the wait at `L1217` in e4 names the releaser that the prediction named. The scalings behind the inverse root cost 0.4 us a unit with the old scores (e12), 0.7 predicted.

**"Ends: 3 us in all."** This is the step that failed most. Of the feed-forward's move it priced only what stays uncovered at the end of the layers; that the same instructions stand beside other work of other units in every one of 24 units it left unpriced. Measured in the kernel before: 165 us (e13), of which 56 are the gelu's table loads; in the changed kernel the loads alone cost 48 us (e19). By its own method, one unit in order of time, it could have been seen in part: in the trace of before the gelu's 4.2 us of ScalarE stand beside the queries' inverse root, and the feed-forward's root stands clear of the first scaling of keys; four steps on neither is so.

**"Light half: 5 x 0.60 at TensorE's pace, since the others have room."** e4 had about 0.75 us less a part and gave back 1.6 us a unit of 8 x 0.75 = 6.0, where five parts at 0.60 should have given 3.0. The prediction named this as the likeliest failing, the chain through the softmax; a share of 97% had hidden it.

**"4 for norms, before 16"** counted the one DMA as issues saved. It costs 41 us in after, 23 in before, for it runs on about 4 of the 16 engines. **"A DMA lands 2.2 us after its issue starts"** was read from one plain load in an idle row [rows 11]; in after, 5.3 and 7.0 us stand in the chain.

**"Hidden by 0.8 us."** A relay's DMA took 0.60 us to issue (median; 0.75 taken), and still the relays cost 53 us, 2.2 a unit. Rival 2 had the right engine and sign. Its place, the first score, waits only 6.8 us in 800 in after, where the norms and the windows of values behind the relays are late first; with the norms in four (e1) it waits 20.2 us in 800, 2.1 a unit, just what the relays cost there. Even so rival 2 had 2556 us: it is one of four losses.

**"The exchange costs nothing extra."** Its copies take 0.50 us each (0.45 taken), and 36 us reach the end: an engine with 34% idle time can still stand in the way at one step.

**Not seen at all.** That ScalarE's copy of values waits for the windows of the tile before: 11.7 us in 800 before, 51.0 after, with those DMAs behind the relays and landing late; and that the granted clock falls where TensorE stands, which makes every wait dearer (up to 127 us more busy time than e4 for the same instructions). In e5 and e9, without relays, no engine waits for a DMA between 600 and 1400 us: the direct copy itself makes nobody wait for a DMA, the relays ahead of its DMAs do.

## What to carry to other kernels

In a schedule that several units share, a step that is moved by its whole length doesn't keep its surroundings: look at which long piece of which other engine it stands beside now (modulo the period), in every unit, before pricing the tail. Look also at what waits for that engine: here a VectorE piece held a DMA queue, and the queue held two more engines. A long piece can be nearly free in one interval and paid in full in the next; the load of a function table cost 0.1 us a time in one interval and 1.2 in the next. And when every engine's busy time stays while the span grows, take the change apart by edits in the old kernel: the share of the chain says who is waited for, not which edit did it.

## What the runs showed of the hardware

- Matmuls of 64 rows by 32 columns of weights in eight tiles at once, float32: 64 instructions in 0.86 us with the last one's 0.22, so 10 ns each; the old form of 32 rows by 32 columns took (1.48 - 0.22) / 127 = 10 ns each as well, for twice as many. Between these two forms the number of instructions set the time, not their rows. The Trainium skill, TensorEngine Tiling (Array Packing), Restrictions and Gotchas, says that different row tiles can't access one PSUM bank at the same time, which lets one expect a loss in after, where both write to each bank; it takes 0.86 us there and 0.86 with a bank for each (e4), so no run shows the loss.
- A DMA with a source of [4, 32, 512] kept the 16 engines busy for a share of 0.26 while it ran alone, and its full cost to the kernel was 41 us in after and 23 in before.
- The granted clock fell to 0.56 over a stretch of 5 us in which TensorE was busy for 0.84 us, and stayed at 0.50 until 947 us, though TensorE worked again from 944.2. Its mean from 600 to 1400 us was 1.00 in before and e4, 0.95 in e13 and e9, 0.91 in after.
- A load of ScalarE's function table took 1.28 us each time, and a pair of them cost the kernel 0.2, 2.0 or 2.3 us, by what stood beside it (e17, e19, e18).
